# Turning the quantized rows of a gated block by DMA instead of on TensorE, inverse roots by a power on GpSimd, and the first feed-forward tile a slot sooner

## The chip, the cores and the metric

One core of a Trainium2 chip runs the whole program. The metric is the device time of one execution in microseconds (us). The engines are TensorE (PE), VectorE (DVE), ScalarE (ACT), GpSimd (POOL) and SyncE (SP), which only issues DMAs here. Each works through its own instructions in order and waits on semaphores.

## The reference, cut to what matters

```python
x = x + tanh(g_xattn) * xattn(layernorm(x), ctx)      # 32 batches, 112 queries, 375 keys, 256 wide, 16 heads
x = x + tanh(g_ffn) * ffn(layernorm(x))

def layernorm(x): return (x - mean) / sqrt(var + 1e-5)
def act_quant(x):                                     # per row, 8 bits
    scale = 127 / max|x|
    return clip(round(x * scale), -128, 127) / scale
def ffn(x):                                           # weights are ternary levels times one scale
    gate = silu(act_quant(x) @ w_gate.T)              # 256 -> 1024
    up = act_quant(x) @ w_up.T
    return act_quant(gate * up) @ w_down.T            # 1024 -> 256
```

The attention takes two softmaxes for each batch and head: one whose statistics go through a small network that gives a temperature, and one with that temperature.

## The kernel before, in words

The attention is written as a pipeline over slots. `t` counts slots, `n, p = divmod(t, 8)`; a slot carries two of the 16 heads of a batch, and the work of several batches is interleaved at fixed lags. `timeline` (defined for all engines) walks the slots from -16 to 310 and calls each engine's `slot(t)`. The feed-forward stage works on 28 tiles of 128 rows. Its steps are `tile(s)`: after the slots named in the table BETWEEN come tiles 0 to 7, and after the last slot the others. All engines follow this one order, and an engine that waits in a slot holds up all that stands behind it.

Before the products of the feed-forward stage each tile has to be normalized, rounded to 8-bit levels and turned (the 256 features must lie on partitions). The tiles go through that in groups of two, 14 groups, of which 12 (`TAILED`) are worked at the end of the attention, one every two slots from t = 258 (`X_AT`), and two late (`LATE_AT`), between the tiles. For group i the steps are: SP loads the rows (`load_group`, L470, slot 255+2i); POOL subtracts the mean (`centre_group`, L741 and L750, slot 257+2i); DVE finds the largest value, its scale and inverse, and rounds (`x_group`, L1021 to L1030, slot 259+2i); POOL makes the levels in bf16 (`quant_group`, L760, slot 260+2i); PE transposes four 128x128 blocks into PSUM (`transpose_group`, L1517, slot 261+2i); DVE copies them out (`copy_group`, L1046, slot 262+2i). Two buffers alternate for the centred rows (`fxn`, shown as ex) and two for the levels (`fxq`, shown as qp). The turned levels of the first 24 tiles stay in SBUF (`xqt`, in kp, kf and ctxt).

The inverse root of the variances is not needed for the rounding. It only scales the gate and the up product. DVE adds epsilon (L1004), ACT takes the square roots (L1181 for 22 tiles at slot 263, L1294 for the last 6 at tile step 9), and DVE takes the reciprocal (L1009) and makes the two scales (L1012 to L1015, `rows_scale`, slot 282 and step 18).

What else runs in these slots, for the last batches: PE does the second scores of one batch (L1401) and the products with the values (L1380), each freed by the exponentials of ACT (L1218). One bank of PSUM, p_m, is shared by the value projection (L1439, copied by DVE L902), the output projection (L1447, slot p = 3, read by DVE L928, slot p = 4) and the transposition back of the output (L1465, slot p = 5, read by DVE L934 and L938). PE waits with each until DVE has read the one before. The turned output of batch m5 goes through the "ride" (PE L1351, DVE copy L959, slot p = 2). POOL guards it first (L697 to L702, slot p = 7) and prepares the residual (L644).

A feed-forward tile n is: gate product (L1524, PSUM p_s0), silu on ACT (L1278), up product (L1524, p_s1), their scaled product on DVE (L1063) and its row maximum (L1068), rounding on ACT or POOL (L1289, L780), levels on POOL (L785), a transposing DMA of 128x1024 on SP (L546), the down product (L1556), and the scaled result plus the residual (L1271, L792 or L1084, L550). The gate product of tile n waits for the silu of tile n-1, the up product for L1063 of tile n-1.

```python
BETWEEN = {SLOTS * (B + 3) + 4: 0, SLOTS * (B + 3) + 6: 1, SLOTS * (B + 3) + 7: 2, ...
```

With B = 32 and SLOTS = 8 these are slots 284, 286 and 287.

Of the kernel before, what the change touches and what calls it, by code (L numbers as in the profile page):

```python
# [14 lines left out]
P = 128  # L15
# [23 lines left out]
SLOTS = 8  # L39
# [28 lines left out]
def gated_block(nc, x_d, ctx_d, cst, out_d):  # L68
# [6 lines left out]
    with es:  # L75
# [68 lines left out]
        rstd2, vpe2, sdev2 = sb("rstd2", [P, TILES]), vpe, sdev  # L144
# [81 lines left out]
        last_ride = p_t[1][:, 0:C * SQ].rearrange("p (c q) -> p c q", c=C)  # L226
# [8 lines left out]
        def ride_of(t, m5):  # L235

            return last_ride if m5 == B - 1 else tail_ride if t >= TAIL else ride[t % 2]

        def p_xq(i):

            home = p_s[0].ap().bitcast(BF16).rearrange("p b k -> p (b k)") if i < EARLY_GROUPS else p_t[1].ap().bitcast(BF16)
            return home[:, 0:GROUP * D].rearrange("p (g c r) -> p g c r", g=GROUP, c=C)
# [34 lines left out]
        s_bn2, s_ln2, s_sq2 = sem("s_f_bn"), sem("s_f_ln"), sem("s_f_sqrt")  # L277
        s_gl = [sem(f"s_f_x_group{i}") for i in range(2)]
        s_ag, s_gx, s_gr, s_gq, s_gt, s_gc, s_gs = (sem(f"s_f_x_{i}") for i in ("means", "chain", "rounded", "quant", "transposed", "copied", "scales"))
# [99 lines left out]
        BETWEEN = {SLOTS * (B + 3) + 4: 0, SLOTS * (B + 3) + 6: 1, SLOTS * (B + 3) + 7: 2, SLOTS * (B + 4) + 1: 3, SLOTS * (B + 4) + 2: 4, SLOTS * (B + 4) + 5: 5, SLOTS * (B + 5) + 4: 6, SLOTS * (B + 6) + 4: 7}  # L379
        X_AT, SQ_AT = TAIL, 9  # L380
        VAR_AT, SQRT_AT, RSTD_AT, RSTD_LATE = SLOTS * B + 6, SLOTS * B + 7, SLOTS * (B + 3) + 2, 18
# [29 lines left out]
        def _(sp):  # L411
# [59 lines left out]

            def slot(t):
# [93 lines left out]
        def _(pool):  # L566
# [7 lines left out]
            pool.wait_ge(s_prp, PRP_LN2)  # L574

# [35 lines left out]
            def slot(t):  # L611
# [122 lines left out]
                if i is not None:  # L734
                    centre_group(i)

# [15 lines left out]

            def quant_group(i):
# [4 lines left out]
                if i >= 2:  # L758
                    pool.wait_ge(s_gt, count(1, i - 2, 1))
                nc.gpsimd.tensor_scalar(fxq[:, i % 2], fxn[:, i % 2], 1.0, -ROUND, ALU.mult, ALU.add).then_inc(s_gq, 1)  # L760

            def tile(s):
# [38 lines left out]
        def _(dve):  # L801
# [89 lines left out]
            def slot(t):  # L891
# [101 lines left out]
                i = group_at(t, 4)  # L993
                if i is not None:
                    copy_group(i)
# [10 lines left out]
            def rows_scale(first, end, j):  # L1006

                dve.wait_ge(s_sq2, j + 1)
                nc.vector.reciprocal(rstd2[:, first:end], sdev2[:, first:end]).then_inc(s_ln2, 1)  # L1009
                dve.wait_ge(s_ln2, count(3, j, 2))  # L1010
                dve.wait_ge(s_gx, count(3, end // GROUP))
                nc.vector.tensor_tensor(rstd2[:, first:end], rstd2[:, first:end], xsc[:, first:end], ALU.mult).then_inc(s_ln2, 1)  # L1012
                dve.wait_ge(s_ln2, count(3, j, 3))
# [19 lines left out]
            def copy_group(i):  # L1033

                dve.wait_ge(s_gt, count(1, i, 1))
                if i == EARLY_GROUPS:
                    dve.wait_ge(s_vmm, 3 * B)
                if i == 0:
                    dve.wait_ge(s_kp2, count(2, B - 1, 2))
                    for b in (B - 2, B - 1):  # L1040
                        dve.wait_ge(s_kst[b % KRING], ring_count(192, b, KRING))
                for g in range(GROUP):
                    k = GROUP * i + g
                    if k >= GROUP * TAILED:
                        dve.wait_ge(s_u, count(1, k - GROUP * TAILED, 1))
                    last = nc.vector.tensor_copy(xqt(k), p_xq(i)[:, g])  # L1046
                last.then_inc(s_gc, 1)

            def tile(s):
                if s == SQ_AT:  # L1050
# [3 lines left out]
                if s - 6 in LATE_AT:  # L1054
# [552 lines left out]
```

## Time and profile before

| | us |
|---|---|
| time, median of 3 runs (787.66 to 788.53) | 788.13 |
| the profiled execution, its time | 786.88 |
| its span, from the first to the last instruction | 785.0 |
| busy: PE, DVE, ACT, POOL | 707.7, 702.0, 672.5, 506.1 |
| mean granted TensorE clock, share of full | 0.951 |

The span is what the profile's positions are counted in. The attention runs alone until about 640 us. From there to 684 us its tail runs beside the levels of x, and from 686 us on the feed-forward tiles. In the rows a number in square brackets is the idle time of the engine just before the instruction, with what ended it. SPq is the queue of SP: its rows are the issues of DMAs, not the transfers.

### The profile page before, as it was taken

Reading aid. Unit: us, or ns where it says so; the run is one execution under the profiler, and the core shown is the slowest. Engines: PE = TensorE matmul, PEld = TensorE weight load, DVE = VectorE, ACT = ScalarE, POOL = GpSimd, SP = SyncE. Lnnn points to the kernel's source line nnn. Section 1 sums busy time; section 2 is a strip of 40 time slices with the busy share of each in tenths; the row PEclk is TensorE's granted clock in tenths of the full one; section 3 lists DMA queues with packets and bytes.
Section 4 is the critical chain, followed back from the end, with each engine's and each line's share of the span. In section 5 each row is a group of like instructions: output and inputs, shape, how many; then the busy total and the mean of one; then the engine's idle time right before and its main releaser. Section 6 shows DMA issues by size and latency. Waiting matters only on the chain.

```text
span 785.0 us, 20889 instructions
## 1 busy us (share of the span) xinstructions
PE 707.7 (90%) x7127; PEld 479.5 (61%) x7127; DVE 702.0 (89%) x1432; ACT 672.5 (86%) x1440; POOL 506.1 (64%) x1004
## 2 busy tenths in 40 slices
PE   7557899989999999999999999999999888879896
PEld 5334566767676766666666666676766566634453
DVE  5779799979899999998999999899999887889995
ACT  1469799999999999989999999999999987559884
POOL 4747657667777776766767676767675146546873
PEclk9667599999999999999999999999999999999998
DMA  9897856465567575667565758565755023238887
GB/s 213 191 256 165 189 140 134 115 124 132 138 125 146 123 145 127 147 118 154 118 151 125 151 120 142 125 154 115 153 111 116 13 73 101 67 74 183 184 178 193
DMA packets 148886, 108.49 MB, mean 138 GB/s; under 512 B 56991, under 2 KB 145183, under 8 KB 148767
## 3 DMA queue, kind: packets, MB, share of 16 engines
q1 hardware_dynamic: 143630, 101.98, 59.7%
q10 hardware_dynamic: 5152, 5.19, 2.7%
q8 instruction: 57, 0.93, 0.5%
q14 instruction: 47, 0.39, 0.2%
HBM read 49.54 MB, written 12.85 MB: 79 GB/s over the span
## 4 chain that ended last, share of the span: by engine, by line
PE 46%; ACT 20%; DVE 14%; issue 10%; POOL 7%; DMA 1%; ACTq 1%; SPq 0%; POOLq 0%; DVEq 0%
PE p_m L1458 9%; PE p_o L1380 8%; ACT ex L1228 7%; PE p_s L1360 7%; ACT pt L1218 6%; PE p_t L1401 6%; PE p_m L1439 5%; DVE stats L950 3%; PE p_m L1447 3%; DVE nm L969 2%; PE p_m L1431 2%; ACT L1218 2%; ACT L1254 2%; POOL kst L785 2%; PE p_m L1465 2%
## 5 line engine op out<-in xcount | busy, mean ns | idle before, releaser
L1228 ACT ACTIVATE ex<-p_s,nm 112x375 f32<-112x375 f32 x512 | 275.0, 616 | 12.4 <-DVE nm L969 12.4
L1218 ACT ACTIVATE pt<-p_t,ct 128x336 f32<-128x336 f32 x488 | 244.9, 574 | 29.1 <-PE p_t L1401 26.6
L950 DVE BATCH_NORM_STATS2 stats<-ex 112x6 f32<-112x375 f32 x512 | 252.4, 534 | 1.8 <-ACT ex L1228 1.8
L969 DVE TENSOR_REDUCE nm<-p_s 112x2 f32<-112x750 f32 x256 | 235.9, 922 | 2.3 <-PE p_s L1360 2.2
L1360 PE MATMUL p_s<-kst,qst 96*112 96x375 bf16 x512 | 156.1, 351 | 13.7 <-ACT ex L1228 7.7
L1401 PE MATMUL p_t<-qst,kst 99*128 99x112 bf16 x1464 | 115.3, 214 | 4.9 <-ACT pt L1218 4.2
L1401 PEld LDWEIGHTS p_t<-qst,kst 99*128 99x128 bf16 x1464 | 91.4, 98 | 43.9 <-issue 19.4
L1439 PE MATMUL p_m<-wv_sb,ctxt 128*128 128x256 f32 (+1 forms) x384 | 107.7, 404 | 5.0 <-DVE on L938 3.2
L1380 PE MATMUL p_o<-pt,va 128*32 128x112 f32 (+1 forms) x3072 | 101.6, 265 | 0.5 <-ACT ex L1228 0.5
L1458 PE MATMUL p_m<-ctxt,wk_sb 128*128 128x375 f32 x240 | 94.8, 519 | 1.7 <-DVE qf L918 1.1
L1360 PEld LDWEIGHTS p_s<-kst,qst 96*112 96x112 bf16 x512 | 67.0, 140 | 46.0 <-ACT ex L1228 36.3
L1380 PEld LDWEIGHTS p_o<-pt,va 128*32 128x32 f32 (+1 forms) x3072 | 70.3, 110 | 28.7 <-issue 26.7
L1439 PEld LDWEIGHTS p_m<-wv_sb,ctxt 128*128 128x128 f32 (+1 forms) x384 | 67.2, 191 | 20.9 <-DVE va L902 8.7
L902 DVE TENSOR_TENSOR va<-p_m,bv_sb 128x256 f32<-128x256 f32 (+1 forms) x96 | 39.9, 416 | 28.6 <-PE p_m L1439 27.8
L585 POOL TENSOR_SCALAR kp<-kf 128x375 bf16<-128x375 f32 x63 | 32.7, 520 | 47.3 <-ACT kf L1161 47.3
L1458 PEld LDWEIGHTS p_m<-ctxt,wk_sb 128*128 128x128 f32 x240 | 45.0, 201 | 28.0 <-DVE x L928 7.7
L591 POOL TENSOR_TENSOR kp<-kf,kp 128x375 bf16<-128x375 f32 x63 | 55.2, 877 | 5.3
L587 POOL TENSOR_TENSOR kf<-kf,kp 128x375 f32<-128x375 f32 x63 | 55.0, 872 | 5.3
L1524 PE MATMUL p_s<-wq,kp 128*128 128x512 bf16 x168 | 43.1, 386 | 7.3 <-DVE kst L1063 5.9
L1431 PE MATMUL p_m<-xnt,wq_sb 128*128 128x112 f32 x256 | 40.1, 306 | 1.3 <-DVE xnt L966 1.2
L1063 DVE SCALAR_TENSOR_TENSOR kst<-p_s,usc,kst 128x1024 f32<-128x1024 f32 x28 | 35.9, 1282 | 5.0 <-ACT kst L1278 4.3
L785 POOL TENSOR_SCALAR kst<-kst 128x1024 bf16<-128x1024 f32 (+1 forms) x28 | 28.8, 1029 | 15.8 <-ACT kst L1289 15.6
(189 smaller groups left out, 1162.8 us busy)
## 6 DMA issues: line engine op xcount, KB each, us to landing
kst<-kp SPq DMA_DIRECT2D x378, 93.8 KB, 3.5
ctxt<-ctxt_dram SPq DMA_DIRECT2D x32, 375.0 KB, 4.2
qbounce<-qp SPq DMA_DIRECT2D x32, 168.0 KB, 2.5
qst<-qbounce SPq DMA_DIRECT2D x32, 168.0 KB, 3.6
qst<-qbounce SPq DMA_DIRECT2D x32, 112.0 KB, 3.4
xm<-x_dram SPq DMA_DIRECT2D x32, 112.0 KB, 2.3
x_dram<-x SPq DMA_DIRECT2D x32, 112.0 KB, 1.9
xt<-x_dram SPq DMA_DIRECT2D x28, 128.0 KB, 3.2
```

The costliest lines, as they stand in the source:

```text
L587: nc.gpsimd.tensor_tensor(kf[:, c], kf[:, c], hi, ALU.subtract).then_inc(s_kx, 1)
L591: nc.gpsimd.tensor_tensor(lo, kf[:, c], mid, ALU.subtract).then_inc(s_kp2, 1)
L950: last = nc.vector.bn_stats(stats[:, nb % RING, 2 * pb + i], ex[0:SQ, 2 * (t % 2) + i, :])
L969: nc.vector.tensor_reduce(nm[:, n % RING, 2 * p:2 * p + 2], p_s[t % 2][0:SQ, :, 0:SK], axis=AX.X, op=ALU.max, negate=True).then_inc(s_max, 1)
L1218: nc.scalar.activation(pt[:, (2 * r + i) % 8], st_home(r, i)[:, 0:KC * SQ].rearrange("k (c q) -> k c q", c=KC), ACT.Exp, scale=ct[:, nr % ...
L1228: nc.scalar.activation(ex[0:SQ, 2 * ((t - 1) % 2) + i, :], p_s[(t - 1) % 2][0:SQ, i, 0:SK], ACT.Exp, bias=nm[:, ne % RING, h:h + 1]).then_ ...
L1360: scores = mm(p_s[t % 2][0:SQ, i, 0:SK], qst[n % KRING][0:STACK, h, :], kst[n % KRING][0:STACK, h, 0:SK], start=True, stop=True)
L1380: last = mm(o_acc[VW * i:VW * (i + 1), grp, :], va[ng % VRING][0:KEYS[c], c, 4 * grp + i, :], pt[0:KEYS[c], (2 * (g - 1) + i) % 8, c, :], ...
L1401: last = mm(st_home(r, i)[:, c * SQ:(c + 1) * SQ], kst[nr % KRING][:, h, c * KR:(c + 1) * KR], qst[nr % KRING][:, h, :], start=True, stop= ...
L1431: last = mm(p_m[:, c * SQ:(c + 1) * SQ], wq[:, k, c * P:(c + 1) * P], xnt[:, k, :], start=(k == 0), stop=(k == C - 1))
L1439: last = mm(p_m[0:KEYS[ch], 0:D], ctxt[:, v % CRING, k, ch * KR:ch * KR + KEYS[ch]], wv[:, k, :], start=(k == 0), stop=(k == C - 1))
L1458: last = mm(p_m[:, 0:SK], wk[:, k, c * P:(c + 1) * P], ctxt[:, f % CRING, k, :], start=(k == 0), stop=(k == C - 1))
```

## The change

The levels of a group are turned by two transposing DMAs on SP, which write straight to `xqt`. PE's transposes and DVE's copies of all 14 groups go. PSUM p_s0 is free earlier, and the turned output of the last batch but one rides in p_t0 and not in p_s0. Tile 0 stands after slot 283 and not after slot 284, and waits only for its own group. The inverse roots come from one power (exponent -0.5) on POOL, 128x22 at slot 263 and 128x6 at tile step 9; ACT's two square roots and DVE's two reciprocals go. `rows_scale` moves from slot 282 to slot 280.

```diff
-            return last_ride if m5 == B - 1 else tail_ride if t >= TAIL else ride[t % 2]
+            return last_rides[m5 % 2] if m5 >= B - 2 else tail_ride if t >= TAIL else ride[t % 2]
...
-        BETWEEN = {SLOTS * (B + 3) + 4: 0, SLOTS * (B + 3) + 6: 1, ...
+        BETWEEN = {SLOTS * (B + 3) + 3: 0, SLOTS * (B + 3) + 6: 1, ...
-        X_AT, SQ_AT = TAIL, 9
-        VAR_AT, SQRT_AT, RSTD_AT, RSTD_LATE = SLOTS * B + 6, SLOTS * B + 7, SLOTS * (B + 3) + 2, 18
+        X_AT, LATE_POW_AT = TAIL, 9
+        VAR_AT, POW_AT, RSTD_AT, RSTD_LATE = SLOTS * B + 6, SLOTS * B + 7, SLOTS * (B + 3), 18
...
+            def turn_group(i):                        # SP, slot 261 + 2i and tile steps 14 and 17
+                if i == 0:
+                    sp.wait_ge(s_kp2, count(2, B - 1, 2))
+                    for b in (B - 2, B - 1):
+                        sp.wait_ge(s_kst[b % KRING], ring_count(192, b, KRING))
+                if i == EARLY_GROUPS:
+                    sp.wait_ge(s_vmm, 3 * B)
+                sp.wait_ge(s_gq, count(1, i, 1))
+                for g in range(GROUP):
+                    k = GROUP * i + g
+                    if k >= GROUP * TAILED:
+                        sp.wait_ge(s_u, count(1, k - GROUP * TAILED, 1))
+                    sp.dma_start_transpose(xqt(k), fxq[:, i % 2, g]).then_inc(s_gt[i % 2], 16)
...
+            def inverse_roots(first, end, j):         # POOL
+                pool.wait_ge(s_exponent, 1)
+                pool.wait_ge(s_ln2, count(2, j, 1))
+                nc.gpsimd.tensor_tensor(rstd2[:, first:end], vpe2[:, first:end], less_half[:, 0:1].to_broadcast([P, end - first]), ALU.pow).then_inc(s_pw2, 1)
...
             def quant_group(i):
                 if i >= 2:
-                    pool.wait_ge(s_gt, count(1, i - 2, 1))
+                    pool.wait_ge(s_gt[i % 2], ring_count(16 * GROUP, i - 2, 2))
...
             def rows_scale(first, end, j):
-                dve.wait_ge(s_sq2, j + 1)
-                nc.vector.reciprocal(rstd2[:, first:end], sdev2[:, first:end]).then_inc(s_ln2, 1)
-                dve.wait_ge(s_ln2, count(3, j, 2))
+                dve.wait_ge(s_pw2, j + 1)
...
-            def copy_group(i):                        # DVE, with its calls
-                    last = nc.vector.tensor_copy(xqt(k), p_xq(i)[:, g])
...
-                if t == SQRT_AT:                      # ACT, and the same at tile step 9
-                    nc.scalar.activation(sdev2[:, 0:EARLY_TILES], vpe2[:, 0:EARLY_TILES], ACT.Sqrt).then_inc(s_sq2, 1)
...
-                    if m5 == B - 1:                   # PE, before the turned output
-                        pe.wait_ge(s_e2, 2 * SLOTS * B)
-                        pe.wait_ge(s_gc, TAILED)
+                    if m5 >= B - 2:
+                        pe.wait_ge(s_e2, 2 * SLOTS * B - (2 if m5 == B - 2 else 0))
...
-            def transpose_group(i):                   # PE, with its calls
-                pe.wait_ge(s_gq, count(1, i, 1))
-                if i > 0:
-                    pe.wait_ge(s_gc, count(1, i))
-                        last = nc.tensor.transpose(p_xq(i)[:, g, c, :], fxq[:, i % 2, g, c * P:(c + 1) * P], identb[:, :])
...
             def tile(s):                              # PE
-                    pe.wait_ge(s_gc, count(1, n // GROUP, 1))
+                    pe.wait_ge(s_gt[n // GROUP % 2], ring_count(16 * GROUP, n // GROUP, 2))
                     if n == 0:
-                        pe.wait_ge(s_gc, EARLY_GROUPS)
-                        pe.wait_ge(s_otc, B - 1)
+                        pe.wait_ge(s_e1, 2 * SLOTS * B)
+                        pe.wait_ge(s_otc, B - 2)
```

## Rows read from the trace of the kernel before

**Rows 1.** Stretches: busy us of each engine, clock, DMA share, in the tail.

```profile
660.00:680.00 20.00, 17.17 (x280) 13.73 (x276) 16.13 (x56) 12.17 (x27) 12.50 (x29) 0.91 0.36 110
```

**Rows 2.** The chain that ended last, in order of time, 658 to 687 us.

```profile
658.39 0.40 DVE kp L1046 x2
...
669.02 0.33 PE p_s L1517 x4
...
675.48 0.39 DVE kp L1046 x2
...
678.14 0.62 POOL qp L760
...
681.93 0.70 DVE xmax L1021
...
686.25 0.43 PE p_t L1517 x4
```

**Rows 3.** Timeline around the first square root, ACT and POOL.

```profile
650.84 1.28 ACT L1181 ACT_TABLE_LOAD   x1
...
652.38 1.28 ACT L1218 ACT_TABLE_LOAD   x1
...
654.91 0.32 POOL L634 TENSOR_SCALAR ltc<-lt 128x32 f32<-128x32 f32 x1 [1.80 <-ACT lt L1186]
```

**Rows 4.** Timeline around the first two feed-forward tiles.

```profile
684.49 1.77 PE L1447 MATMUL p_m<-wo_sb,ot 128*112 128x256 f32 x4 [0.64 <-DVE ot L959]
...
686.29 0.48 DVE L928 SCALAR_TENSOR_TENSOR x<-p_m,tg_sb,xm 112x256 f32<-112x256 f32 x1 [0.73 <-PE p_m L1447]
...
686.47 2.73 PE L1524 MATMUL p_s<-wq,kp 128*128 128x512 bf16 x8
...
688.38 1.11 ACT L1278 ACTIVATE kst<-p_s,gsc 128x1024 f32<-128x1024 f32 x1 [1.45 <-PE p_s L1524]
...
689.04 0.60 PE L1465 MATMUL p_m<-ident_sb,oa 128*112 128x128 f32 x4
689.53 1.28 DVE L1063 SCALAR_TENSOR_TENSOR kst<-p_s,usc,kst 128x1024 f32<-128x1024 f32 x1 [2.32 <-ACT kst L1278]
...
689.64 1.02 PE L1524 MATMUL p_s<-wq,kp 128*128 128x512 bf16 x4
690.85 1.22 DVE L1068 TENSOR_REDUCE hmax<-kst 128x1 f32<-128x1025 f32 x1
...
693.13 1.27 DVE L1063 SCALAR_TENSOR_TENSOR kst<-p_s,usc,kst 128x1024 f32<-128x1024 f32 x1
```

**Rows 5.** Stretches of 2 us: an idle PE and the clock after it (columns of Rows 1).

```profile
662.00:664.00 2.00, 0.46 (x9) 0.30 (x6) 1.86 (x7) 1.11 (x3) 0.95 (x3) 1.00 0.71 224
664.00:666.00 2.00, 1.86 (x5) 1.32 (x6) 0.48 (x3) 0.00 (x0) 1.68 (x5) 0.57 0.44 132
```

**Rows 6.** Timeline of the late square root and of one late copy.

```profile
718.00 1.28 ACT L1278 ACT_TABLE_LOAD   x1
...
720.44 1.28 DVE L1063 SCALAR_TENSOR_TENSOR kst<-p_s,usc,kst 128x1024 f32<-128x1024 f32 x1 [1.21 <-ACT kst L1278]
...
738.71 0.48 DVE L1046 COPY kp<-p_t 128x256 bf16<-128x256 bf16 x2
```

**Rows 7.** Line L546, SP's transposing DMAs of 128x1024: issue in ns, landing in us.

```profile
L546 SPq DMA_TRANSPOSE kst<-kst x28: 1237/1237/2392, 698.4 to 777.3; - x28
...
DMA to landing us min/median/max: 3.1/3.3/5.1
```

**Rows 8.** SP's timeline: a load of one group, two DMAs.

```profile
661.28 0.93 SPq L470 DMA_DIRECT2D ctxt<-x_dram  x2
```

**Rows 9.** Timeline, POOL's small operations and a DVE operation beside one.

```profile
645.90 0.24 POOL L680 TENSOR_TENSOR fd<-fa 112x32 f32<-112x32 f32 x1 [0.44 <-DVE fa L944]
...
682.45 0.72 POOL L644 TENSOR_TENSOR xm<-xm,bo_sb 112x256 f32<-112x256 f32 x1
...
682.65 0.54 DVE L1023 TENSOR_SCALAR xsc<-xmax 128x2 f32<-128x2 f32 x1
...
683.23 0.17 DVE L1025 RECIPROCAL xinv<-xsc 128x2 f32<-128x2 f32 x1
```

More of the change, by code:

```diff
@@ L225, in gated_block @@
         V_COPY_AT = {7: (0, V_LAG), 0: (1, V_LAG + 1), 1: (2, V_LAG + 1)}
-        last_ride = p_t[1][:, 0:C * SQ].rearrange("p (c q) -> p c q", c=C)
+        last_rides = [p_t[i][:, 0:C * SQ].rearrange("p (c q) -> p c q", c=C) for i in range(2)]
         tail_ride = p_s[0][:, 1, 0:C * SQ].rearrange("p (c q) -> p c q", c=C)
@@ L276, in gated_block @@
         s_neg, s_cen = sem("s_f_means_negated"), sem("s_f_x_centred")
-        s_bn2, s_ln2, s_sq2 = sem("s_f_bn"), sem("s_f_ln"), sem("s_f_sqrt")
+        s_bn2, s_ln2, s_pw2 = sem("s_f_bn"), sem("s_f_ln"), sem("s_f_inverse_roots")
+        s_exponent = sem("s_f_exponent")
         s_gl = [sem(f"s_f_x_group{i}") for i in range(2)]
-        s_ag, s_gx, s_gr, s_gq, s_gt, s_gc, s_gs = (sem(f"s_f_x_{i}") for i in ("means", "chain", "rounded", "quant", "transposed", "copied", "scales"))
+        s_ag, s_gx, s_gr, s_gq, s_gs = (sem(f"s_f_x_{i}") for i in ("means", "chain", "rounded", "quant", "scales"))
+        s_gt = [sem(f"s_f_x_transposed{i}") for i in range(2)]
         s_g, s_u, s_sg, s_h, s_hmx, s_hrec, s_hinv, s_hr, s_hq = (sem(f"s_f_{i}") for i in (
@@ L536, in slot @@
                     load_group(i)
+                i = group_at(t, 3)
+                if i is not None:
+                    turn_group(i)
             def tile(s):
@@ L559, in tile @@
                     load_group(LATE_AT[s + 1])
+                if s - 4 in LATE_AT:
+                    turn_group(LATE_AT[s - 4])
             timeline(slot, tile)
@@ L574, in _ @@
             pool.wait_ge(s_prp, PRP_LN2)
+            nc.gpsimd.memset(less_half[:, :], -0.5).then_inc(s_exponent, 1)
             def split_k(b, c):
@@ L1031, in x_group @@
                     last.then_inc(s_gr, 1)
-            def copy_group(i):
[L1035 to L1045, printed above, removed]
-                    last = nc.vector.tensor_copy(xqt(k), p_xq(i)[:, g])
-                last.then_inc(s_gc, 1)
             def tile(s):
-                if s == SQ_AT:
+                if s == LATE_POW_AT:
                     rows_var(EARLY_TILES, TILES, 1)
@@ L1291, in tile @@
                     round_group(LATE_AT[s - 2])
-                if s == SQ_AT:
-                    act.wait_ge(s_ln2, 4)
-                    nc.scalar.activation(sdev2[:, EARLY_TILES:TILES], vpe2[:, EARLY_TILES:TILES], ACT.Sqrt).then_inc(s_sq2, 1)
             timeline(slot, tile)
@@ L1501, in slot @@
                     mm(p_t[0][:, 0:3], ones, wsum[:, 1, :], start=False, stop=True).then_inc(s_tot, 1)
-                i = group_at(t, 3)
-                if i is not None:
-                    if i == 0:
-                        pe.wait_ge(s_e1, 2 * SLOTS * B)
-                    if i == EARLY_GROUPS:
-                        pe.wait_ge(s_e2, 2 * SLOTS * B - 2)
-                    transpose_group(i)
-            def transpose_group(i):
-                pe.wait_ge(s_gq, count(1, i, 1))
-                if i > 0:
-                    pe.wait_ge(s_gc, count(1, i))
-                for g in range(GROUP):
-                    for c in range(C):
-                        last = nc.tensor.transpose(p_xq(i)[:, g, c, :], fxq[:, i % 2, g, c * P:(c + 1) * P], identb[:, :])
-                last.then_inc(s_gt, 1)
             def product(dst, wm, n):
```

23 lines of the change are left out of this document (7 added, 16 removed).

## The prediction, made before the change was run

> **What bounds it now.** I began with the stretches. In the tail of the attention no engine is full. From 660 to 680 us PE is busy for 17.2 of 20 us and DVE for 16.1 [rows 1]. So I read the chain that ended last. From 655 to 684 us it runs mostly through DVE, from one group of x to the next, and the copies that the change removes lie on it in four places, 0.40 us each; the rows show the first and the last [rows 2]. PE's transposes of the levels lie on it twice, 0.33 and 0.43 us. Then I read the two places where ACT switches tables for a square root [rows 3, 6], and the start of the first tiles [rows 4]. From there DVE goes through L1063 and L1068 of each tile, 1.28 and 1.22 us, nearly without a gap, so what shifts the early tiles shifts the end.
>
> **The change, step by step.** Times are against the profiled execution, 786.88 us (span 785.0), which lies 1.25 us under the median of the runs, 788.13. A minus is a gain.
>
> *First square root: -1.5.* ACT loads the table for the root at 650.84 and the one for the exponentials at 652.38 [rows 3]. The second load is needed anyhow, after the gelu. It moves to the place of the first: 1.54 us. Scores for the next exponential lie ready, while PE, DVE's copy of the values and POOL's L634 (idle 1.80 us) wait for ACT here. So nearly all of it counts; the ends are 0 and -1.6. Next late is PE's value projection, which comes as much earlier.
>
> *Copies and transposes of groups 0 to 10: -1.9.* The chain holds 4 x 0.40 + 0.33 + 0.43 = 2.4 us of them [rows 2]. I don't take all of it. By my walk through the slots DVE reaches group 10 1.9 us earlier. Then POOL leads: from L760 of group 9 at 678.14 its own work (levels, guards, centring of group 11) leads to L1021 at 681.93 [rows 2], 3.8 us in which nothing is removed. That leaves some 1.5 us at L1447; the 0.43 us of PE's transposes ahead of tile 0 come on top. Ends: -0.4 if all else is hidden, and -4.4 = -11 x 0.40 if every copy counts. The walk is nearest to the chain, so I take -1.9. `rows_scale` at slot 280 falls into DVE's wait for POOL ahead of 681.93 and costs nothing there; without that wait it would cost some 0.6 us.
>
> *Tile 0 a slot sooner: +2.9.* PE has nothing in slot 284, so on PE tile 0 starts where it did, right after L1447. On DVE it is otherwise: L928 stands in slot 284 and now falls behind tile 0. L928 empties p_m, and PE's L1465 in slot 285 waits for that; tile 1 stands behind L1465 on PE. Counted from the gate product of tile 0 at 686.47 [rows 4]: L1068 of tile 0 ends at +5.6, L928 at +6.0, L1465 (0.60) at +6.7. The gate product of tile 1 and its silu follow, 1.02 and 1.1 us, and L1063 of tile 1 starts at about +8.9. Before it started at 693.13, which is +6.7. That is +2.2 at full clock. PE is idle from +2.7 to +6.1, and after a shorter idle stretch the granted clock was 0.57, which means mostly the lower level, 1.2 GHz [rows 5]. At that level L1465 and the gate product take 1.3 us more together: +3.5. Taken half and half, +2.9. DVE waited 2.32 us for the silu before L1063 of tile 0 [rows 4]; L928 lay in that wait for nothing, and its cover is gone. ACT's copy of the output (slot 284) falls behind the silu of tile 0 too, but is done at about +3.6 and hidden. The ends are 0 and +3.6.
>
> *Late square root: -1.2.* DVE waits 1.21 us at 720.44 for the silu behind the second table load [rows 6]. Both loads go, the up and gate products are ready by then. Ends 0 and -1.3.
>
> *Late groups 12 and 13: -0.7.* Two pairs of copies on DVE, 0.40 us each as they overlap [rows 6], and a reciprocal of 0.2 us. PE is nearly full behind 745 us, so I take 0.7 of 1.0.
>
> *SP: 0.* Each group adds two issues of a transposing DMA. The trace has only larger ones, 1.24 us an issue and 3.3 us to landing [rows 7]; the lower end is 0.46 us, a plain load [rows 8]. At the upper end a group costs SP 0.93 + 2 x 1.24 = 3.4 us, with other transfers some 3.7, as much as a group takes now. The turned levels land at most 1.24 + 3.3 = 4.6 us after POOL's L760; the first that wait for them are L760 two groups on (some 7 us later) and tile 0. Queued behind `turn_group` on SP are the load of group i+4 and the stores of x, with several slots to spare. In tile steps 14 and 17 SP gets up to 2.5 us more; a down product is issued three tiles (8 us) behind its DMA, which needs 4.6, so 3.4 us cover it. Lost, if the cover were gone: some 1 us each.
>
> The Trainium skill (VectorE: DVE Perf Modes, the three transpose paths) gives 1309 ns for a 128x128 transposition by DMA against 390 ns on TensorE. A group has four such blocks, 5.2 us by that figure, more than the 3.7 us that a group takes. The trace speaks against adding them up: the 128x1024 DMA has eight blocks and lands in 3.3 us [rows 7].
>
> *Power on POOL: 0.* No row shows one. From below it is as an ordinary operation of 128x32, 0.24 us [rows 9]. From above I take twenty such operations in a row, 4.8 us. I take 1 us, nearer to the lower end, because only 22 columns are worked. It stands behind the centring of group 3 at 652.3. POOL has about 1.5 us until it would hold up ACT or group 4: its wait of 1.80 us at 654.91 [rows 3] gets shorter as ACT comes sooner, but group 4 is centred 1.5 us before DVE takes it. At 1 us it is hidden; at 4.8 us it costs 3.3.
>
> Beside that stands a contention: L1023 took 0.54 us next to POOL's L644, and L1025, of the same size, 0.17 [rows 9]. The Trainium skill (SBUF — State Buffer, "SBUF: two separate sides") says that GpSimd and some DVE operations take one port pair as an exclusive lock, for the whole instruction. By that rule the power would hold DVE for up to its own length, 1 us at my value, and the sum would be 1 us worse; without it, nothing is added.
>
> **Sum.** -1.5 - 1.9 + 2.9 - 1.2 - 0.7 = -2.4, so 784.5 for the profiled execution and 785.7 for the median. About 0.2% (1.6 us) is what a measurement of this kernel can tell from no change.
>
> **Rivals.**
> A. *Tile 0 costs nothing*, because L928 after all comes in time or the gap is caught up by DVE. Against: the order of the code, and DVE without gaps behind. Then -5.3: 782.8. Chance 0.17.
> B. *The tail is paced by PE and ACT*, the copies lie in DVE's waits, and the clock falls at tile 1: -1.5 - 0.4 + 3.5 - 1.2 - 0.7 = -0.3, 787.8, no change. For: PE is busier than DVE in rows 1. Chance 0.22.
> C. *A long power*, on the other side. It stands at slot 263 on POOL, ahead of the levels of group 2. Above 1.5 us every further us delays group 4 on DVE and POOL's L634, and so ACT. It turns the gain at about 4 us and is slower by over 0.2% from 5.5 us on. At 8 us: -2.4 + 6.5, 792.2. Against: ordinary POOL operations of this size take 0.24 us [rows 9]. Chance 0.10.
> D. *The small transposing DMAs take as long as the large ones and don't overlap*: 2 x 3.3 = 6.6 us a group [rows 7]. L760 two groups on waits, and the tail runs at 6.6 us a group and not at 3.7. Eleven groups by 2.9 us is +32, with the rest some 818. Against: in the feed-forward stage SP issues the large ones every 2.8 us or so and PE still keeps its pace. Chance 0.03. With the 5.2 us a group by the figure of the Trainium skill (VectorE: DVE Perf Modes, the three transpose paths) it would be 802.
> The forecast has 0.48, its own range 784.2 to 787.2.
>
> **Numbers.** Faster by over 0.2% is below 786.55: most of the forecast (0.38) and A: 0.55. Within: the rest of the forecast above that line (0.08), B and the edges: 0.30. Slower: C, D and a tail of B: 0.15. The range of 8 in 10 leaves out D, most of C and the best of A: 782.0 to 789.5.
>
> **What would show it.** No table load between the gelu and the next exponential at about 651, and none near 716. The gate product of tile 0 some 3.4 us earlier than 686.47, and close behind L1447 as before. L928 behind L1068 of tile 0, PE idle for about 3 us in between, and 9 to 10 us from the gate product of tile 0 to L1063 of tile 1. POOL's power about 1 us, and SP's issues at or under 1.24 us, with no wait of POOL's L760 for a DMA. I am wrong if DVE's pace per group doesn't change, if the power is over 2 us, if L760 waits for a landing, or if tile 1 follows tile 0 in under 7 us.

## The result, and the profile after

The changed kernel takes 796.39 us (median of 4 runs, 794.0 to 797.41) against 787.89 for the kernel before on the same chip (784.18 to 788.53). That is 8.5 us slower by the medians, a ratio of 1.0108. The ratio taken run against run is 1.0141 [1.0103, 1.0179], which is 11 us. Of the experiments below, two of the twelve executions of e9 were slow (942.82 and 1062.40 us, at a mean granted clock of 0.65 and 0.60) and are left out of its median. The forecast was 785.7 in a range of 782.0 to 789.5, so the time lies outside the range, on the side that had a chance of 0.15. The profiled execution took 795.86 us, with a span of 794.0.

I read the trace in the order of the prediction's steps. In the changed file the levels' DMAs are line L482, the loads of a group L467, POOL's levels L786 and its centring L770, and the power L777. First the two transposing DMAs of a group, by their source line:

```profile
L482 SPq DMA_TRANSPOSE kp<-qp x21: 1173/1246/2201, 644.2 to 752.3; - x21
...
  POOL qp L786: 8.3, 8
...
DMA to landing us min/median/max: 2.3/2.3/4.2
```

Issuing one costs SP 1.24 us, as much as the four times larger DMA of the feed-forward stage [rows 7]. It lands in 2.3 us, not 3.3. POOL waited for them eight times, 8.3 us in all, which the prediction had named as a sign that it is wrong. SP's timeline in the tail of the attention (x2 means two DMAs in one row):

```profile
658.53 2.46 SPq L482 DMA_TRANSPOSE kp<-qp  x2
661.04 0.58 SPq L508 DMA_DIRECT2D xm<-x_dram  x1
661.66 0.43 SPq L512 DMA_DIRECT2D x_dram<-x  x1
662.13 0.92 SPq L467 DMA_DIRECT2D ctxt<-x_dram  x2
663.09 2.47 SPq L482 DMA_TRANSPOSE kp<-qp  x2
665.66 0.52 SPq L543 DMA_DIRECT2D xt<-x_dram  x1
666.23 0.91 SPq L467 DMA_DIRECT2D ctxt<-x_dram  x2
667.18 2.95 SPq L482 DMA_TRANSPOSE kp<-qp  x2
```

Each row starts within 0.1 us of the end of the one ahead of it. SP issues like this from here to 691 us. From the transposes of group 2 at 653.85 to those of group 11 at 688.75 a group takes 3.9 us. In the kernel before, POOL's levels of the same groups came every 3.5 us. So SP has become the bound, and POOL waits for it in both of its steps, for the transposes ahead of L786 and for the loads queued behind them on SP ahead of L770:

```profile
670.07 0.94 POOL L770 TENSOR_SCALAR ex<-ctxt,xinv 128x256 f32<-128x256 f32 x2 [1.48 <-DMA ctxt<-x_dram]
...
675.25 0.62 POOL L786 TENSOR_SCALAR qp<-ex 128x512 bf16<-128x512 f32 x1 [1.21 <-DMA kp<-qp]
...
677.76 0.94 POOL L770 TENSOR_SCALAR ex<-ctxt,xinv 128x256 f32<-128x256 f32 x2 [1.71 <-DMA ctxt<-x_dram]
```

The start of the first two tiles, where [rows 4] stand for the kernel before (timeline of all engines; L956 is the old L928, L1068 the old L1063, L1463 the old L1465, L1504 the gate and up products):

```profile
688.17 2.85 PE L1504 MATMUL p_s<-wq,kp 128*128 128x512 bf16 x8
...
691.27 1.28 DVE L1068 SCALAR_TENSOR_TENSOR kst<-p_s,usc,kst 128x1024 f32<-128x1024 f32 x1 [5.06 <-ACT kst L1280]
692.59 1.22 DVE L1073 TENSOR_REDUCE hmax<-kst 128x1 f32<-128x1025 f32 x1
693.72 0.47 DVE L956 SCALAR_TENSOR_TENSOR x<-p_m,tg_sb,xm 112x256 f32<-112x256 f32 x1
...
694.45 1.07 PE L1463 MATMUL p_m<-ident_sb,oa 128*112 128x128 f32 x4 [3.43 <-DVE x L956]
...
699.03 1.28 DVE L1068 SCALAR_TENSOR_TENSOR kst<-p_s,usc,kst 128x1024 f32<-128x1024 f32 x1 [2.75 <-PE p_s L1504]
```

The order is the one that was forecast: tile 0's h, then x, then PE's L1463, then tile 1. It took 10.86 us from the gate product of tile 0 to L1068 of tile 1, where it was 6.66 before. The gate product itself came 1.7 us later than before, not 3.4 earlier. Of the 10.86 us, 3.10 lie between the gate product and tile 0's own L1068, about as before (3.06), and 7.76 between that and tile 1's, where it was 3.60. PE worked at half its clock through much of this (stretches of 4 us, columns of [rows 1]; the clock is the third number from the end):

```profile
680.00:684.00 4.00, 1.85 (x26) 1.24 (x26) 2.56 (x6) 1.28 (x1) 2.94 (x7) 0.50 0.50 141
684.00:688.00 4.00, 1.68 (x8) 1.22 (x5) 2.11 (x6) 0.00 (x0) 1.98 (x4) 0.50 0.35 82
...
696.00:700.00 4.00, 4.00 (x10) 1.31 (x9) 1.25 (x2) 1.11 (x1) 1.49 (x3) 0.50 0.19 55
```

A granted clock of 0.50 is the lower level, 1.2 GHz. PE had stood still for 4.96 us until 682.15, for POOL's L720.

The power, and what stood beside it and behind it (three timelines, of POOL, DVE and ACT):

```profile
649.30 3.90 POOL L777 TENSOR_TENSOR rstd<-vpe,less_half 128x22 f32<-128x22 f32 x1
653.20 0.62 POOL L786 TENSOR_SCALAR qp<-ex 128x512 bf16<-128x512 f32 x1
653.80 0.33 POOL L652 TENSOR_SCALAR ltc<-lt 128x32 f32<-128x32 f32 x1
```

```profile
651.52 0.42 DVE L930 TENSOR_TENSOR va<-p_m,bv_sb 119x256 f32<-119x256 f32 x1 [1.71 <-PE p_m L1437]
651.86 0.68 DVE L1044 TENSOR_REDUCE xmax<-ex 128x2 f32<-128x512 f32 x1
```

```profile
654.16 0.32 ACT L1195 ACTIVATE ct<-ltc,ln_sb 128x32 f32<-128x32 f32 x1 [2.08 <-POOL ltc L652]
```

It took 3.90 us, not 1. The two table loads for the square roots are gone, as forecast: the load for the exponentials comes directly behind the gelu, at 647.92, and there is none near 716 or after it. In the kernel before POOL waited for ACT at this place, 1.80 us [rows 3]; now ACT waits for POOL, 2.08 us.

The last rows of output (DVE's timeline, then SP's):

```profile
784.65 0.48 DVE L1089 SCALAR_TENSOR_TENSOR kst<-p_o,ysc,kst 128x256 f32<-128x256 f32 x1 [2.07 <-DMA out_dram<-kst]
787.27 0.48 DVE L1089 SCALAR_TENSOR_TENSOR kst<-p_m,ysc,kst 128x256 f32<-128x256 f32 x1 [2.13 <-DMA out_dram<-kst]
...
791.33 0.48 DVE L1089 SCALAR_TENSOR_TENSOR kst<-p_m,ysc,kst 128x256 f32<-128x256 f32 x1 [1.04 <-PE p_m L1536]
```

```profile
783.61 1.24 SPq L561 DMA_TRANSPOSE kst<-kst  x1
784.89 0.63 SPq L565 DMA_DIRECT2D out_dram<-kst  x1
785.56 0.44 SPq L572 DMA_DIRECT2D kst<-x_dram  x1
786.11 1.24 SPq L561 DMA_TRANSPOSE kst<-kst  x1
```

Here too SP issues one row behind the other. A tile costs it 2.5 us (783.61 to 786.11). The last transposition of h is issued at 786.11, 10.3 us after the start of the last L1073 (775.85); in the kernel before it was issued at 777.26, 5.9 us after the same instruction (L1068 there, 771.32). I call this distance SP's lag. It is a better measure of the queue than the stretch up to the last row, since behind the last transposition the last down product follows, which takes 1.05 us or 1.89 according to the clock it meets.

### The profile page after: what moved, and what is told of

Its sections match the earlier page's. It is cut to its first block and busy times, and to the rows that moved or that the text cites. A ratio compares the mean times of both kernels' runs of the same rounds, so it can differ in the third digit from the quotient of the medians.

```text
span 794.0 us, 20760 instructions
## 1 busy us (share of the span) xinstructions
PE 706.0 (89%) x7071; PEld 474.2 (60%) x7071; DVE 699.3 (88%) x1402; ACT 667.3 (84%) x1435; POOL 511.8 (64%) x1007
## 5 line engine op out<-in xcount | busy, mean ns | idle before, releaser
L1230 ACT ACTIVATE ex<-p_s,nm 112x375 f32<-112x375 f32 x512 | 274.9, 616 | 12.3 <-DVE nm L997 10.8
L1358 PE MATMUL p_s<-kst,qst 96*112 96x375 bf16 x512 | 154.5, 348 | 13.4 <-ACT ex L1230 7.3
L1504 PE MATMUL p_s<-wq,kp 128*128 128x512 bf16 x168 | 45.1, 404 | 4.6 <-DVE kst L1068 3.6
L1280 ACT ACTIVATE kst<-p_s,gsc 128x1024 f32<-128x1024 f32 x28 | 31.0, 1109 | 19.3 <-PE p_s L1504 19.1
L1068 DVE SCALAR_TENSOR_TENSOR kst<-p_s,usc,kst 128x1024 f32<-128x1024 f32 x28 | 35.9, 1283 | 9.6 <-ACT kst L1280 6.4
L1445 PE MATMUL p_m<-wo_sb,ot 128*112 128x256 f32 x128 | 37.6, 418 | 3.1 <-DVE ot L987 3.1
```

The lines of the kernel that those rows point to most:

```text
L1230: nc.scalar.activation(ex[0:SQ, 2 * ((t - 1) % 2) + i, :], p_s[(t - 1) % 2][0:SQ, i, 0:SK], ACT.Exp, bias=nm[:, ne % RING, h:h + 1]).then_ ...
L1358: scores = mm(p_s[t % 2][0:SQ, i, 0:SK], qst[n % KRING][0:STACK, h, :], kst[n % KRING][0:STACK, h, 0:SK], start=True, stop=True)
L1504: last = nc.tensor.matmul(dst[:, hf, :], xqt(n)[:, k, :], wq8[wm][:, k * F + hf * 512:k * F + (hf + 1) * 512], start=(k == 0), stop=(k == ...
```

## The experiments

To see where the time goes I took anchors from the timelines of DVE and PE in every run: DVE's sum x of slot 260, the first gate product (G), the products L1063/L1068 of tiles 1, 9, 10, 19 and 27, and the last row that DVE adds. Stretches in us. From tile 19 to 27 all runs need 22.2 to 22.4, so that column is left out. The moment of slot 260 itself varies by 5.6 us from one profile to another, and the anchors leave this out; ahead of it only e8, e10, e11 and e12 have something changed (the early power, slot 249). The last column is the way from slot 260 to the last row as a whole.

| run | x 260 to G | G to tile 1 | 1 to 9 | 9 to 10 | 10 to 19 | 27 to last row | x 260 to last row |
|---|---|---|---|---|---|---|---|
| before | 41.39 | 6.66 | 23.37 | 3.94 | 27.35 | 12.34 | 137.26 |
| after | 46.02 | 10.86 | 23.73 | 2.74 | 26.60 | 16.80 | 149.18 |
| e1 power | 42.53 | 6.24 | 23.36 | 2.74 | 26.97 | 12.30 | 136.38 |
| e2 turning | 45.96 | 6.89 | 23.82 | 3.95 | 26.64 | 14.39 | 143.87 |
| e3 slot | 40.35 | 8.90 | 23.37 | 3.95 | 27.32 | 11.70 | 137.82 |
| e4 turning, power | 46.71 | 6.75 | 23.58 | 2.74 | 26.60 | 15.84 | 144.44 |
| e5 | 45.70 | 6.90 | 23.71 | 3.95 | 27.02 | 13.27 | 142.76 |
| e6 | 39.52 | 6.90 | 24.06 | 3.94 | 26.89 | 12.15 | 135.70 |
| e7 | 40.29 | 6.00 | 23.37 | 3.95 | 27.31 | 12.27 | 135.41 |
| e8 | 39.58 | 5.61 | 23.37 | 2.74 | 27.29 | 11.61 | 132.42 |
| e9 | 39.20 | 10.59 | 23.86 | 2.74 | 26.61 | 13.28 | 138.50 |
| e10 | 36.81 | 6.89 | 23.84 | 2.74 | 26.60 | 13.81 | 132.92 |
| e11 | 39.12 | 6.51 | 23.36 | 2.74 | 27.30 | 11.44 | 132.69 |
| e12 | 39.12 | 6.90 | 23.48 | 2.74 | 27.30 | 12.25 | 134.01 |

Each experiment is timed beside the kernel before, in three sets (e1 to e4, e5 to e8, e9 to e12), and its ratio is taken within its set. The stretches are of one execution each. Set against the kernel before, their sum and the medians disagree by up to 2.9 us (e8: 4.8 us less by the stretches, 1.9 by the medians), so a difference of 1 or 2 us in one stretch needs the rows behind it, or the medians, to be believed.

### Each part alone (e1 to e4; before: 785.87)

**e1**, the kernel before with the roots alone changed:

```diff
-                nc.scalar.activation(sdev2[:, 0:EARLY_TILES], vpe2[:, 0:EARLY_TILES], ACT.Sqrt).then_inc(s_sq2, 1)
...
+                nc.gpsimd.tensor_tensor(rstd2[:, first:end], vpe2[:, first:end], less_half[:, 0:1].to_broadcast([P, end - first]), ALU.pow).then_inc(s_pw2, 1)
```

> The kernel before with the roots alone changed: POOL's power in place of ACT's square roots, the rest untouched. Theory: the power takes 3.9 us for 22 columns and holds up POOL's levels of group 2 and L634 by some 2.4 us more than its cover of 1.5; the two table switches give back 1.5 and 1.2. So -1 to +1.5 us against the kernel before. Rival (the power is what made the change slow): +5 us or more.

782.89 us, ratio 0.9970 [0.9942, 0.9998]: 3.0 us less by the medians, more than the theory's best case of 1, and the rival (slower by 5 us or more) is refuted. By the stretches it is only 0.9 us.

**e2**, the changed kernel with the roots back on ACT and DVE and tile 0 back behind slot 284, so that of the three parts only the turning by DMA is left (with what goes with it: the rides, `rows_scale` at slot 280, and tile 0 waiting for its own group alone).

> The changed kernel with the roots back on ACT and DVE and tile 0 back after slot 284: the transposing DMAs alone. Theory: SP is short of time with 1.24 us for each small DMA, whatever its size; loads and levels come late in the tail (+2 to +4 us), and in the feed-forward stage SP is left some 4.5 us behind at the end, less 0.9 for the copies. So +5 to +8 us against the kernel before. Rival (as predicted, SP has cover): -2.6 us.

791.87 us, ratio 1.0076 [1.0048, 1.0104]: 6.0 us more, as the theory had it.

**e3**, the kernel before with the place of tile 0 alone changed:

```diff
-        BETWEEN = {SLOTS * (B + 3) + 4: 0,
+        BETWEEN = {SLOTS * (B + 3) + 3: 0,
... (the rest of both lines is the same)
```

> The kernel before with tile 0 after slot 283 and nothing else. Theory: L928 falls behind tile 0 on DVE, PE's L1465 and tile 1 wait for it, and the clock is low: +2.2 to +4.2 us, read between the gate product of tile 0 and L1063 of tile 1 (6.7 us before, 9 to 11 here). Rival A (tile 0 costs nothing): 0 us.

788.38 us, ratio 1.0032 [1.0004, 1.0061], and 2.2 us more from G to tile 1, both as the theory had it.

**e4**, the changed kernel with that line undone.

> The changed kernel with tile 0 back after slot 284. Theory: the distance from the gate product of tile 0 to L1068 of tile 1 falls from 10.9 to about 7 us, and the time by 2.2 to 4.2 us against the changed kernel, to 792 to 794. If SP's queue is what sets the end whatever the tiles do, the time falls by less than 1 us.

791.30 us, ratio 1.0074 [1.0046, 1.0102]. From G to tile 1 it is 6.75 us, as expected; the time falls by 5.1 us against the changed kernel, more than the 2.2 to 4.2 that I expected.

So the turning costs 6.0 us, the slot 2.5, and the power brings 3.0 (medians). The sum is +5.5; the whole is +8.5 by its medians and +11 by its ratio, so 3 to 5.6 us are missing. By the stretches the whole is +11.9 and the three parts +6.3. The missing 5.6 lie in two places: 2.2 from G to tile 1 and 3.1 behind tile 27.

Of the latter, half shows in e4. Turning and power together cost 5.4 where the parts add to 3.0. Tiles 9 to 10 are 1.21 us shorter in e4 than in e2, the late square root, as forecast, but the stretch behind tile 27 is 1.45 us longer, 15.84 against 14.39. The power is not to blame for that (in e1, without the turning, the end is as long as before, 12.30), and neither are the tiles that come sooner: from the transposition of tile 11, the last ahead of the first late group, to that of tile 16 SP's lag is the same in e4 and e2 to 0.4 us. It parts at one issue of e4, that of tile 17, which takes 2.80 us and not 1.24:

```profile
752.94 2.80 SPq L561 DMA_TRANSPOSE kst<-kst  x1
```

From there to the end e4 has 1.3 to 1.6 us more lag than e2 (10.2 against 8.7 at the last tile). Such long issues, 0.5 to 1.6 us over the usual, stand in every run from 725 us on, one to three of them, the kernel before included (2.39 us at 761.09). Where SP has time to spare they vanish; here they stay until the end. The changed kernel has three of them, and its last down product falls in the low clock as well, which is another 0.84 us against e4:

```profile
789.40 1.89 PE L1536 MATMUL p_m<-wq,kst 128*128 128x256 bf16 x8 [0.57 <-DMA kst<-kst]
```

```profile
783.94 1.05 PE L1536 MATMUL p_m<-wq,kst 128*128 128x256 bf16 x8 [1.09 <-DMA kst<-kst]
```

The first row is of the changed kernel, the second of e4.

### Is it SP's queue? (e5, e6; before: 785.01)

**e5**, e2 with the last two groups turned by PE and copied by DVE again (SP's call is dropped, as shown; PE's and DVE's come back):

```diff
-                if s - 4 in LATE_AT:
-                    turn_group(LATE_AT[s - 4])
```

> The turning alone (e2_turning_only), but the last two groups (24 to 27) are turned by PE and copied by DVE again, as in the kernel before; groups 0 to 11 stay on SP. Theory 1, SP's queue is behind in the last tiles: each late group takes 2.48 us of issuing from SP, so without them the stretch from the last product of FFN tile 27 to the last row of output goes from 14.39 us (turning alone) back to about 12.3 (before: 12.34), and the time falls by 2 to 3 us against the turning alone (791.87), to about 789 to 790; the loss ahead of the first gate product stays. Rival, the end is later only because the early part is: the stretch stays at 14.4 us and the time at 791.9.

790.79 us, ratio 1.0081 [1.0049, 1.0113]. The end is 13.27 us, between what the theory (12.3) and the rival (14.4) expected, and the time that of e2. That looks as if the late groups explain about half of the longer end. SP's lag says more: without them it is that of the kernel before up to tile 26 (6.2 us there, 6.1 before, 9.1 in e2), so it was they that filled the queue. Of the 0.93 us by which the end is still longer than before, 0.7 come from one long issue (2.07 us) at the last tile but one:

```profile
776.42 2.07 SPq L564 DMA_TRANSPOSE kst<-kst  x1
```

The 0.4 us that the groups cost PE and DVE (27.02 against 26.64) goes against the gain.

**e6**, e2 with one DMA for a group in place of two; the homes of the turned levels are cut at even tiles for it (16 in kp, 4 in kf, 4 in ctxt):

```diff
-                for g in range(GROUP):
-                    k = GROUP * i + g
...
-                    sp.dma_start_transpose(xqt(k), fxq[:, i % 2, g]).then_inc(s_gt[i % 2], 16)
+                sp.dma_start_transpose(home[:, at * D:(at + GROUP) * D].rearrange("p (c r) -> p c r", c=GROUP * C),
+                                       fxq[:, i % 2].rearrange("p g d -> p (g d)")).then_inc(s_gt[i % 2], 16)
```

> The turning alone, with one transposing DMA for each group (128x512) in place of two (128x256 each); the homes of the levels are cut at even tiles for it. Theory 1, the issue costs SP 1.24 us for each DMA whatever its size: SP gets 1.24 us a group back, 15 us over groups 0 to 11, POOL no longer waits for the transposing and load DMAs, the stretch from the last x of the attention to the first gate product falls from 16.32 us to 12 to 13 (before: 11.47), the end from 14.39 to about 12.5, and the time falls by 4 to 6 us against the turning alone (791.87), to 786 to 788. Rival, the issue costs by the block of 128x128 (1.24 us for two blocks, so 2.4 for four): issue 2.3 to 2.5 us, nothing changes, 791 to 792. A third: the issue is cheap but a large transpose lands later (3.3 us where the small one took 2.3, since PE waits for the landing), which gives back about 1 us once.

785.22 us, ratio 0.9993 [0.9970, 1.0016], 6.6 us under e2 with the same bytes transposed and a little more than the 4 to 6 that I expected. Its source line and its SP queue:

```profile
L486 SPq DMA_TRANSPOSE kp<-qp x10: 1194/1195/1596, 647.6 to 743.5; - x10
...
who waited for it (us, times):
...
DMA to landing us min/median/max: 2.4/2.8/4.5
```

```profile
664.88 0.90 SPq L471 DMA_DIRECT2D ctxt<-x_dram  x2
665.83 1.20 SPq L486 DMA_TRANSPOSE kp<-qp  x1
667.34 0.80 SPq L471 DMA_DIRECT2D ctxt<-x_dram  x2
668.19 1.19 SPq L486 DMA_TRANSPOSE kp<-qp  x1
670.19 1.08 SPq L471 DMA_DIRECT2D ctxt<-x_dram  x2
```

Twice the size costs SP the same 1.20 us. There are gaps in the queue again (667.03 to 667.34, 669.38 to 670.19), and nobody waits for a landing. The way from x of slot 260 to the gate product falls from 45.96 to 39.52 us, and SP's lag at the last tile from 8.7 to 5.9 us, that of the kernel before. That settles it: the loss of the turning was SP's time to issue, 1.24 us for each DMA, and not the transposing. A single landing even became slower, 2.8 us for 2.3. A whole group is down sooner all the same, 2.8 us after its first issue begins and not some 3.6, because the second issue (1.22 us ahead of the last 2.35) is gone; that too is issuing time.

### The place of tile 0 and the power (e7, e8; before: 785.01)

**e7**, e3 with DVE's sum x of slot 284 made at the end of slot 283, ahead of tile 0's product:

```diff
-                if p == 4 and 0 <= m5 < B:
+                def add_residual():
...
+                if p == 4 and 0 <= m5 < B and t - 1 not in BETWEEN:
+                    add_residual()
...
+                if p == 3 and t in BETWEEN:
+                    add_residual()
```

> Tile 0 a slot sooner as in e3_slot_only, but DVE makes the sum x of slot 284 ahead of tile 0's product and not behind it. Theory 1, the loss of e3 (788.38, +2.5 us against 785.87) is PE's wait for that x behind tile 0's h on DVE: without it the stretch from the first gate product to the product of tile 1 falls from 8.90 us to 6.7 or less, and the time is that of before or up to 1 us under it. Rival, the loss is that tile 0's 16 matmuls stand ahead of the last attention work of slot 284 on PE: the stretch stays near 8.9 and the time at 788.

785.60 us, ratio 1.0005 [0.9982, 1.0027]; from G to tile 1 it is 6.00 us, where e3 has 8.90. So the loss of the slot was the x behind tile 0's h, and not tile 0's products ahead of the last attention work on PE. And mended, the slot sooner brings nothing that can be measured.

**e8**, e1 with the early power in two parts, 21 columns in slot 249 and the last in 263 (against e1; not shown: DVE adds the epsilon for the 21 in slot 247):

```diff
+                if t == SQRT_FIRST:
+                    inverse_roots(0, FIRST_TILES, 0)
                 if t == SQRT_AT:
-                    inverse_roots(0, EARLY_TILES, 0)
+                    inverse_roots(FIRST_TILES, EARLY_TILES, 1)
```

> The power alone (e1_power_only), with the 22 early roots in two: 21 columns at slot 249, where POOL is idle for 11.9 us, and the last column at slot 263. Theory 1, in e1 the 3.90 us of power held POOL's queue ahead of the levels and gave back what leaving the square root brought: with the split, POOL's second power is about 0.5 us, x of slot 260 to 268 falls from 16.83 us to 14 to 15.3, and the time is 1 to 2 us under e1 (782.89), about 781 to 782. Rival, POOL catches up by itself within ten slots (e1's next stretch was 1.3 us shorter): nothing is gained, 782.5 to 783.5. Against both: the early power of 3.7 us meets DVE at work in slots 249 to 251 and costs there.

783.07 us, ratio 0.9968 [0.9944, 0.9993]. In this trace the stretch from x of slot 260 to that of slot 268 takes 13.88 us, where e1 takes 16.83 and the kernel before 15.34. But e1 gets half of that back in the next eight slots (13.28 against 14.84), and by their medians the two are the same, as the rival had it. POOL's timeline shows where the power went:

```profile
623.21 3.71 POOL L764 TENSOR_TENSOR rstd<-vpe,less_half 128x21 f32<-128x21 f32 x1
...
652.71 0.59 POOL L764 TENSOR_TENSOR rstd<-vpe,less_half 128x1 f32<-128x1 f32 x1
```

### Put together (e9 to e12; before: 785.72)

**e9**, the changed kernel with e6's edit.

> The changed kernel with one edit, one transposing DMA for each group in place of two. e6 took 6.6 us off the turning alone by this (791.87 to 785.22). Theory 1, the queue of SP is what the changed kernel lost by: the same 6 us or a little more go here (the power has pushed POOL later, so SP is not the only one that is late), and what is left is the price of tile 0's place, 2.5 us, less the 2.4 of the power: 785 to 787 us against 785 to 788 of before. Rival, with SP free POOL's 3.90 us of power ahead of the levels is what the first gate product waits for: the fall is only 3 to 4 us, 788 to 790.

786.89 us, ratio 1.0022 [1.0000, 1.0045]: 9.5 us under the changed kernel by this edit, though the two medians are of different sets. That is in the range of theory 1 and more than the 6 us or a little more that it gave for the fall. From G to tile 1 it still takes 10.59 us. PE's L1468 waits 3.28 us for x, and the twelve products behind it run at a granted 0.57 (692 to 696 us), 0.36 us each, where seven at 0.96 took 0.24 each (e3, 684.89 to 686.56):

```profile
691.81 0.82 PE L1468 MATMUL p_m<-ident_sb,oa 128*112 128x128 f32 x4 [3.28 <-DVE x L961]
692.42 4.28 PE L1509 MATMUL p_s<-wq,kp 128*128 128x512 bf16 x12
```

**e10**, the changed kernel with the edits of e6, e7 and e8.

> The changed kernel with three edits: one transposing DMA a group (e6), DVE's sum x of slot 284 ahead of tile 0's product (e7), and the early power in two parts (e8). If the three are worth here what they were alone (6.6, 2.8 and at most 1 us), it takes 783 to 785 less the late square root, so 782.0 to 784.5, some 1 to 3 us under the kernel before. Rival, the pieces share one bound, DVE and POOL in the last slots of the attention, and do not add: 785 or more, the same as before. Against e11: whether turning by DMA is worth anything once its queue is not in the way.

782.29 us, ratio 0.9956 [0.9934, 0.9978], inside the expected 782.0 to 784.5.

**e11**, the kernel before with the power in two parts, tile 0 a slot sooner and x ahead of it, but the levels turned by PE.

> The kernel before with everything of the change but the turning, and mended: power in two parts, tile 0 a slot sooner, the sum x ahead of its product; levels turned by PE and copied by DVE as before. From the parts: 785.0 less 1.9 (e8) and plus or minus 0.6 (e7), so 782.5 to 783.7. Theory 1, the turning brings nothing even when mended: e11 is as fast as e10 or faster. Rival, taking 34 transposes from PE and 17 copies from DVE brings 1 to 2 us when SP has room: e10 is that much under e11.

782.30 us, ratio 0.9950 [0.9925, 0.9975], as fast as e10: theory 1, the turning brings nothing even when mended, holds.

**e12**, one DMA a group for groups 0 to 11, the late ones by PE, the power in two parts, tile 0 in its old place.

> One transposing DMA a group for groups 0 to 11, groups 12 and 13 by PE and DVE, the power in two parts, tile 0 in its old place (slot 284). In e5 the stretch from the last product of FFN tile 27 to the last row of output fell only from 14.39 us to 13.27. Theory 1, SP's queue at 94 per cent in the tiles was still to blame for half of that: here the stretch is 12.0 to 12.5 us, and the time 781 to 783.5. Rival, the late groups cost SP nothing once they are one DMA each (1.20 us): the end is as in e10, and PE's and DVE's extra work costs 0.3 to 0.7 us in tiles 15 to 19.

781.92 us, ratio 0.9950 [0.9926, 0.9974]. The end is 12.25 us, where theory 1 had it, but not for its reason: SP's lag at the last tile is 6.6 us, that of e5, and what is 1.0 us shorter than in e5 is mostly the last down product, at full clock here (1.05 us for 1.89). The stretch from tile 10 to 19 is 0.7 longer than in e10, as the rival had it.

All three beat both kernels, the one before by 3.4 to 3.8 us and the changed one by 14, and they can't be told apart from each other, nor from e1, the power alone (0.9970). So what they gain is no more, as far as these runs can tell, than what the inverse roots alone bring. The table shows what the turning by DMA is worth once it is mended: e10 is 2.3 us faster than e11 to the gate product and 0.7 us from tile 10 to 19, loses 0.4 up to tile 1 and 0.5 up to tile 9, and 2.4 us behind tile 27 (13.81 against 11.44), of which 1.7 are SP's lag (7.6 us for 5.9). It pays with SP at the end for what it gains on PE and DVE.

## Why the prediction was wrong, step by step

*First square root, -1.5: right.* It shows where nothing else stands in its way: 15.34 to 13.88 us in e8. In the changed kernel, with the power there, the same eight slots take 16.60.

*Copies and transposes, -1.9: right in size, but only with SP out of the way.* e6 has 39.52 for 41.39, -1.9, in one execution each. By the medians even that does not come through (e6: ratio 0.9993, where the forecast for the turning was -2.6 us in all). In the change itself the stretch was 4.6 us longer.

*SP at 0: this step failed.* The turning alone was to bring 2.6 us and costs 6.0 (e2), which is 8.6 of the 10.9 us by which the forecast of -2.4 misses +8.5. I took 1.24 us an issue from the right rows, and reckoned 3.4 to 3.7 us a group, "as much as a group takes now". That number should have rung: an engine at 100% can't be hidden, since its loads and transposes stand in one queue and what POOL waits for is issued behind what it doesn't need. I looked only at whether each landing came in time with an empty queue. For the last tiles I did the same: 3.4 us of cover for one DMA. But SP's queue there needs about 2.5 us of the 2.8 that a tile takes, in the kernel before too (its timeline, with one gap of 0.26 us ahead of the last row):

```profile
767.12 1.24 SPq L546 DMA_TRANSPOSE kst<-kst  x1
768.40 0.61 SPq L550 DMA_DIRECT2D out_dram<-kst  x1
769.06 0.44 SPq L557 DMA_DIRECT2D kst<-x_dram  x1
769.76 1.25 SPq L546 DMA_TRANSPOSE kst<-kst  x1
```

0.3 us a tile are free. A late group's 2.5 us would take eight tiles to be worked off, the second one follows three tiles later, and each long issue takes 0.5 to 1.6 us more. I said that it would cost "some 1 us each" if the cover were gone; the end is 2.1 us longer in e2 and 4.5 in the changed kernel.

*Rival D* (0.03) pointed at the same DMAs by the wrong mechanism. Transposes don't take 3.3 us each one behind the other; they overlap, and the issue is what doesn't. The estimate of 5.2 us a group, worked out from the figure of the Trainium skill (VectorE: DVE Perf Modes, the three transpose paths), did not come either: a group of four blocks lands in 2.8 us in e6.

*Tile 0 a slot sooner, +2.9: right in mechanism, in size partly by luck.* The wait for x is there, and e7 shows that it is the loss. e3 has +2.2 from G to tile 1, which is what I had for full clock, and +2.5 us by the medians. But PE did not run at full clock in e3: behind its wait twelve products took 4.44 us, 0.37 each, and from tile 0's h to tile 1's it is 6.91 us for 3.60, so +3.3. What hid 1.1 of that is that tile 0's own products met the high clock (0.96 from 684 to 686 us, where the kernel before had 0.50 from 686 to 688): from G to tile 0's h it is 1.99 us for 3.06. In the changed kernel they met the low one again, and the whole is +4.2, above my upper end of 3.6. I had reckoned with the clock behind the wait only. PE had stood idle ahead of tile 0 too, and not only because SP was late: e9, with SP relieved, has +3.9, and there PE waited 2.80 us for DVE's copy L992 just before.

*Late square root, -1.2, and late groups, -0.7: right where they stand.* 3.94 to 2.74 and 27.35 to 26.60. In the changed kernel SP's lag at the end, 10.3 us for 5.9, takes more than both.

*Power, 0: too small a price.* It took 3.90 us; my bounds were 0.24 and 4.8, and "nearer to the lower end" had no reason in the rows, which held no power. The sentence for that case (it delays ACT through L634) is what happened: the eight slots from slot 260 take 16.83 us in e1 and 13.88 in e8. The contention that I set beside it did not come. Alone the power did not decide: e1 and e8 gain 3.0 and 1.9 us, and I had 2.7 for the two roots.

What is still open: why parts and whole differ by 3 to 5.6 us is shown for the end (long issues, the clock of the last product) and for tile 0 (its clock) by rows of single profiles, not by runs of their own; what makes an issue long now and then was not looked into, and neither was why tiles 1 to 9 take 0.1 to 0.7 us more with the turning by DMA in all its forms.

## To carry to other kernels

Before moving work to a queue, add up what the queue issues in a period and compare it with the period; that each transfer alone lands in time says nothing. Where a DMA costs the same to issue whatever its size, make it as large as the layout allows: one edit of this kind was worth 6.6 us here. And leave the queue some slack: here 0.3 us a tile was free, and neither the extra issues nor the long ones were worked off before the end.

## What the runs showed that was not expected

- A transposing DMA takes SP 1.2 us to issue for 128x256, 128x512 and 128x1024 alike (1246, 1195 and 1237 ns [rows 7]), and lands in 2.3, 2.8 and 3.3 us. So by these medians a block of 128x128 more costs 0.13 to 0.25 us of landing and nothing of issuing.
- An issue of SP now and then takes 0.5 to 1.6 us longer than its like, in every run one to three times from 725 us on, on transposing and plain DMAs alike (1.87 us at 735.80 for a store and 2.71 at 758.63 for a transposition in the changed kernel).
- POOL's power takes 3.90 us for 22 columns, 3.71 for 21, 1.34 for 6 and 0.59 for one: about 0.16 us a column and 0.4 ahead of it. An addition on POOL of 128x32 took 0.24 us in all [rows 9].
- The power did not hold up DVE. The forecast had set beside it that L1023 took 0.54 us next to POOL's L644 [rows 9]. The same operation inside the power takes 0.17 us, in the changed kernel:

```profile
652.57 0.17 DVE L1046 TENSOR_SCALAR xsc<-xmax 128x2 f32<-128x2 f32 x1
```

  L1044 beside the power took 0.68 us, and its like before the change, beside no power, 0.70 [rows 2]; in e8 DVE went through its statistics and maxima at their usual pace beside the whole 3.71 us:

```profile
623.52 1.01 DVE L965 BATCH_NORM_STATS2 stats<-ex 112x6 f32<-112x375 f32 x2
```

  By the lock that the Trainium skill describes (SBUF — State Buffer, "SBUF: two separate sides") only some DVE operations can be held by GpSimd, those in a two-port mode or with two inputs in SBUF. None with two inputs in SBUF ran beside the power in these rows, and the rows don't show the mode, so the rule is not tested here. One pair of L1053 starts 0.23 us before the end of the power and takes 0.99 us, where the same line takes 0.61 to 0.86 before the change; but it takes up to 1.07 in the changed kernel where no power is near (at 675.20).
